# An LSTM stage of a graph network: the hidden state is computed on ACT, behind each tanh, in place of DVE

## The chip, the cores and the metric

One Trainium2 chip, one core. The metric is the device time of one execution in microseconds (us). Engines are named as the profile names them: PE is TensorE's matmuls, PEld its weight loads, DVE is VectorE, ACT is ScalarE, POOL is GpSimd, SP is SyncE.

## The reference, cut to what matters

The network has four levels, each a graph layer, a linear-attention layer and a feed-forward layer, on 625 nodes of 512 features. The feed-forward layer of the second level is an LSTM that runs over the 625 nodes as over time, with a batch of one:

```
def step(carry, x_t):
    h_prev, c_prev = carry
    combined = concatenate((x_t, h_prev))
    f_t = sigmoid(combined @ W_f + b_f)
    i_t = sigmoid(combined @ W_i + b_i)
    c_tilde = tanh(combined @ W_c + b_c)
    c_t = f_t * c_prev + i_t * c_tilde
    o_t = sigmoid(combined @ W_o + b_o)
    h_t = o_t * tanh(c_t)
    return (h_t, c_t), h_t
```

There are 625 such steps, and each needs the h of the one before. The part with x_t is computed for all nodes ahead of the loop; the part with h_prev is a product of one row of 512 by a 512 x 2048 matrix in each step.

## The kernel before, in words

Everything runs in one program, each engine with its own instruction stream, tied by semaphores. Of the four levels only the LSTM loop is touched. A sigmoid is computed as a tanh: with y = tanh(z/2), sigmoid(z) is (1 + y)/2, and the halves are folded into the weights. So the kernel's h is twice the reference's: h = (1 + y_o) * tanh(c).

The 512 hidden features lie as four columns (chunks) of 128 partitions in `ls_hid`. Two halves f = 0 and f = 1 of the features are treated one after the other, each with two chunks c = 0 and c = 1, so column 2f + c. Four semaphore events per step say that a column of h is new: `ls_h[0]` twice, `ls_h[1]` twice.

PE's step (L1153 to L1167): `seed(0)` and `seed(1)` put the x part of both halves into PSUM (L1143). Then come eight `add(f, c)` (L1149), each of which multiplies column c of h into the sums of half f, as 8 instructions. Their order is written out: (0,0), (1,0), (0,1), (0,2), (0,3), then (1,1), (1,2), (1,3). PE waits for column 0 before the first, for column 1 before (0,1), for column 2 (`ls_h[1]`) before (0,2) and for column 3 before (0,3). `add(0,3)` ends with `ls_full[0]`: half 0's sums are done. `add(1,3)` ends with `ls_full[1]`. `add(1,1)` ends with `ls_used`, column 1 having been read for the last time.

For each half DVE turns the sums from rows into columns: `turn` (L2225) for three of the gates and `turn_o` (L2230) for the output gate. ACT takes tanh of the three gates (L1607) and of the output gate (L1609, into `ls_gate[:, f, 8:10]`). DVE multiplies and adds: `product` (L2236), `cell` (L2241), `halve` (L2246). ACT takes the tanh of c, chunk by chunk, in two instructions with a per-partition bias (L1614, function `cell` on ACT). DVE then makes each column of h (L2255, function `hidden`). ACT's `keep` (L1619) copies the four columns to the output store, after both columns of half 1, and ACT's `pick_step` (L1624) prepares the seed's weights for the next step, at the start of a step.

Each engine handles its instructions in the order in which they are written. On DVE that order is `turn(0)`, `turn_o(0)`, `product(0)`, `cell(0)`, `hidden(0,0)`, `turn(1)`, `hidden(0,1)`, `turn_o(1)`, `halve(0)`, `product(1)`, `cell(1)`, `hidden(1,0)`, `hidden(1,1)`, `halve(1)`. On ACT it is pick, `gates(0)`, `cell(0)`, `gates(1)`, `cell(1)`, keep.

Beside the LSTM steps runs a sort of the 10,000 edges for the next level. In 320 of the 625 steps (two passes of 160) it puts eight small bf16 matmuls behind each step on PE (L1207), in every step one 625-element instruction on ACT behind `keep` (L1638 and L1643 in turn), and one large one on DVE in every second step (L2216). These are called rank steps here, and the other 305 plain steps. Between some of the plain steps stands a longer block of DVE work of the sort (L2339 to L2352 is one).

Of the kernel before, what the change touches and what calls it, by code (L numbers as in the profile page):

```python
# [26 lines left out]
ALU = mybir.AluOpType  # L27
ACT = mybir.ActivationFunctionType
# [176 lines left out]
def network(nc, io, last):  # L205
# [19 lines left out]
    with ExitStack() as ctx:  # L225
        def sb(name, shape, dt=F32):
            return ctx.enter_context(nc.sbuf_tensor(name, shape, dt))

        def sem(name):
            return ctx.enter_context(nc.semaphore(name))  # L230
# [32 lines left out]
        ls_hid = sb("ls_hid", [128, KC])  # L263
        ls_gate = sb("ls_gate", [128, 2, 10])
        ls_pr = sb("ls_pr", [128, 2, 4])
        ls_c = sb("ls_c", [128, 2, 2])
        ls_th = sb("ls_th", [128, 2, 2])
# [37 lines left out]
        ls_out_gate = [sem(f"ls_out_gate{f}") for f in range(2)]  # L305
        ls_prod = [sem(f"ls_prod{f}") for f in range(2)]
        ls_cell = [sem(f"ls_cell{f}") for f in range(2)]
        ls_tanh = [sem(f"ls_tanh{f}") for f in range(2)]
        wh_in = sem("wh_in")
        ls_h = [sem(f"ls_h{f}") for f in range(2)]  # L310
        ls_blank = sem("ls_blank")
        ls_used = sem("ls_used")
# [7 lines left out]
        ls_kept = sem("ls_kept")  # L320
# [89 lines left out]
        def weight(name):  # L410
            n = weight_at[name]
            _, k, w, _ = weights[n]
            return ring[:, n % RING, 0:k * w].rearrange("p (k w) -> p k w", k=k)
# [1069 lines left out]
        def _(act):  # L1483
# [70 lines left out]
            if last >= 3:  # L1554
# [5 lines left out]
                          bias=lambda c: cols[:, cb + c:cb + c + 1])  # L1560
# [18 lines left out]
            if last >= 4:  # L1579
# [8 lines left out]
                for i in range(4 * NT):  # L1588
                    t, j = i // 4, i % 4
# [21 lines left out]
                def cell(f, t):  # L1611
                    act.wait_ge(ls_prod[f], t + 1)
                    for c in range(2):
                        nc.scalar.activation(ls_th[:, f, c:c + 1], ls_pr[:, f, c:c + 1], ACT.Tanh, scale=0.5,  # L1614
                                             bias=ls_pr[:, f, 2 + c:3 + c]).then_inc(ls_tanh[f], 1)

                def keep(t):
                    act.wait_ge(ls_h[1], t * 2 + 4)
                    nc.scalar.activation(ls_out[:, :, bass.ds(t, 1)].rearrange("p c o -> p (c o)"), ls_hid[:, :],  # L1619
                                         ACT.Copy).then_inc(ls_kept, 1)  # L1620
# [5 lines left out]
                def step(t, last=False):  # L1626
                    if not last:
                        pick_step(t + 1)
                    gates(0, t)
                    cell(0, t)  # L1630
                    gates(1, t)
                    cell(1, t)
                    keep(t)
# [46 lines left out]
            if last >= 5:  # L1680
# [7 lines left out]
                          bias=lambda c: cols[:, bq + c:bq + c + 1])  # L1688
# [23 lines left out]
            def col(name, c):  # L1712
                return cols[:, COL_AT[name] + c:COL_AT[name] + c + 1]

            if last >= 6:
# [4 lines left out]
                for j in range(2):  # L1720
                    copy_cols(f"L2f.h{j}", lambda c: h1T[:, 4 * j + c, :], KC, ACT.Relu,
                              bias=lambda c: col("L2_ffn_b1", 4 * j + c))
            if last >= 7:
# [19 lines left out]
                for j in range(10):  # L1743
                    act.wait_ge(*made("L3.less", j // 5 + 1))
                    make(nc.scalar.activation(pT[j], sB[:, j // 5, :], ACT.Identity,
                                              bias=sdl[0:R, j // 5, j % 5:j % 5 + 1]), "L3.low")
# [38 lines left out]
        def _(dve):  # L1785
            st = Steps(dve, dve_step)
            V = nc.vector
# [347 lines left out]
            if last >= 4:  # L2135
# [49 lines left out]
                for i in range(4 * NT):  # L2185
                    t, j = i // 4, i % 4
# [36 lines left out]
                def turn(f, t, u):  # L2223
                    dve.wait_ge(ls_full[f], t + 1)
                    V.transpose(ls_turn[:, f, 2:8, :], ls_sum[u][f][:, 64:256].rearrange("p (g n) -> p g n", g=6)  # L2225
                                ).then_inc(ls_turned[f], 1)

                def turn_o(f, t, u):
                    dve.wait_ge(ls_full[f], t + 1)
                    V.transpose(ls_turn[:, f, 0:2, :], ls_sum[u][f][:, 0:64].rearrange("p (g n) -> p g n", g=2)  # L2230
                                ).then_inc(ls_turned_o[f], 1)

                def product(f, t):
                    dve.wait_ge(ls_sig[f], t + 1)
                    dve.wait_ge(ls_state[f], t + 1)
                    V.scalar_tensor_tensor(ls_pr[:, f, :], ls_gate[:, f, 0:4], 1.0, ls_gate[:, f, 4:8],  # L2236
                                           ALU.add, ALU.mult).then_inc(ls_prod[f], 1)

                def cell(f, t):
                    dve.wait_ge(ls_prod[f], t + 1)  # L2240
                    V.scalar_tensor_tensor(ls_c[:, f, :], ls_pr[:, f, 0:2], 0.5, ls_pr[:, f, 2:4],  # L2241
                                           ALU.mult, ALU.add).then_inc(ls_cell[f], 1)

                def halve(f, t):
                    dve.wait_ge(ls_cell[f], t + 1)
                    V.tensor_scalar(ls_gate[:, f, 6:8], ls_c[:, f, :], 0.5, None, ALU.mult).then_inc(ls_state[f], 1)  # L2246

                def hidden(f, c, t):
                    if c == 0:
                        dve.wait_ge(ls_out_gate[f], t + 1)  # L2250
                    if (f, c) == (0, 0):
                        dve.wait_ge(ls_kept, t + 1)
                        dve.wait_ge(ls_used, t + 1)
                    dve.wait_ge(ls_tanh[f], t * 2 + (c + 1))
                    V.scalar_tensor_tensor(ls_hid[:, 2 * f + c:2 * f + c + 1], ls_gate[:, f, 8 + c:9 + c], 1.0,  # L2255
                                           ls_th[:, f, c:c + 1], ALU.add, ALU.mult).then_inc(ls_h[f], 1)

                def step(t, u, between=None):
                    turn(0, t, u)
                    turn_o(0, t, u)  # L2260
                    product(0, t)
                    cell(0, t)
                    hidden(0, 0, t)
                    turn(1, t, u)
                    hidden(0, 1, t)
                    turn_o(1, t, u)
                    halve(0, t)
                    product(1, t)
                    cell(1, t)
                    if between:  # L2270
                        between()
                    hidden(1, 0, t)
                    hidden(1, 1, t)
                    halve(1, t)

                def rank_pass(k, t0):
                    with dve.Fori(0, ET // 2) as it:
                        for u in range(2):
                            step(it * 4 + (t0 + 2 * u), 0)
                            rank_place(it * 2 + (ET * k + u), u)  # L2280
                            step(it * 4 + (t0 + 2 * u + 1), 1, lambda: rank_put(it * 2 + (ET * k + u), u))

                def steps(a, b):
                    with dve.Fori(0, (b - a) // 2) as it:
                        for u in range(2):
                            step(it * 2 + (a + u), u)
                    if (b - a) % 2:
                        step(b - 1, 0)
# [483 lines left out]
```

## Time and profile before

| what | value |
|---|---|
| median of 3 runs | 4237.9 us (4237.68 to 4247.15) |
| profiled execution | 4236.93 us |
| its span (first to last instruction) | 4235.2 us |
| PE busy | 4087.3 us, 97% of the span |
| DVE busy | 2297.0 us, 54% |
| ACT busy | 1871.1 us, 44% |
| granted TensorE clock, mean | 0.976 |

The median is 1.0 us above the profiled execution, and that is 1.7 us above its span. A row of the page's list of costly groups reads: line, engine, operation, output<-inputs, shapes, count, then total busy time and mean ns of one, then the time for which the engine sat idle ahead of it, with what ended that. The share of PE is high partly because matmuls overlap and their ends are modelled: the start times of a step tell more.

### The profile page before, as it was taken

To read this page: it belongs to the slowest core of one execution; us is meant where nothing else is said; L and a number is where in the kernel's file an instruction comes from. 1 tells how busy PE (TensorE), PEld (TensorE's weight loads), DVE (VectorE), ACT (ScalarE), POOL (GpSimd) and SP (SyncE) were. 2 spreads that over 40 slices of the span, in tenths; PEclk is the share of its full clock that TensorE was granted. 3 is DMA by queue.
4 is the path that set the end of the run, shared out by engine and by line. 5 is a ranking of instruction groups with operands and counts; after the bars stand their busy time and mean duration, and the time that the engine had idled before them with its cause. 6 is when DMAs were issued, how large, how long until landed. Compare 5 with 4: busy or idle time off the path is not lost.

```text
span 4235.2 us, 138876 instructions
## 1 busy us (share of the span) xinstructions
PE 4087.3 (97%) x53914; PEld 2082.5 (49%) x53914; DVE 2297.0 (54%) x10694; ACT 1871.1 (44%) x7115; POOL 458.1 (11%) x452
## 2 busy tenths in 40 slices
PE   9999898999999999999999999999999999987999
PEld 7555454445555444445555444434444477456443
DVE  6444313666666666666666666666666145345212
ACT  0110111577777655577777655555555223030111
POOL 0000001000000123100000022200332100010321
PEclk9999899999999999999999999999999999998999
DMA  3010101630000000000000000000000141110974
GB/s 123 10 55 31 47 30 80 182 113 6 10 0 0 1 2 2 5 0 0 0 0 0 1 2 2 5 0 1 1 1 2 51 112 47 42 61 4 352 283 177
DMA packets 65113, 195.21 MB, mean 46 GB/s; under 512 B 29992, under 2 KB 37871, under 8 KB 49035
## 3 DMA queue, kind: packets, MB, share of 16 engines
q0 software_dynamic: 25824, 105.45, 7.8%
q1 hardware_dynamic: 39181, 88.23, 6.3%
q8 instruction: 78, 1.28, 0.1%
q14 instruction: 30, 0.25, 0.0%
HBM read 159.22 MB, written 34.15 MB: 46 GB/s over the span
## 4 chain that ended last, share of the span: by engine, by line
PE 94%; DVE 4%; ACT 1%; issue 1%; DMA 0%; POOL 0%; POOLq 0%; DVEq 0%; ACTq 0%
PE PS L1149 52%; PE PS L833 23%; PE PS L1432 4%; PE PS L1143 3%; PE PS L925 3%; PE PS L1207 2%; PE PS L1285 1%; PE PS L1333 1%; PE PS L1275 1%; PE PS L1265 1%; PE PS L864 1%; ACT BUF L1494 1%; PE PS L894 0%; DVE stats L1814 0%; PE PS L1428 0%
## 5 line engine op out<-in xcount | busy, mean ns | idle before, releaser
L1149 PE MATMUL PS<-BUF,ls_hid 128*1 128x256 f32 x40000 | 2309.0, 379 | 6.1 <-DVE ls_hid L2255 5.8
L1149 PEld LDWEIGHTS PS<-BUF,ls_hid 128*1 128x1 f32 x40000 | 955.2, 83 | 1155.5 <-DVE ls_hid L2255 299.1
L2225 DVE STREAM_TRANSPOSE ls_turn<-PS 128x192 f32<-128x192 f32 x1250 | 479.3, 383 | 466.5 <-PE PS L1149 466.2
L1614 ACT ACTIVATE ls_th<-ls_pr 128x1 f32<-128x1 f32 x2500 | 601.2, 287 | 102.1 <-DVE ls_pr L2236 0.2
L833 PE MATMUL PS<-ring,BUF 128*125 128x512 f32 (+1 forms) x1120 | 476.0, 583 | 13.0 <-ACT BUF L1494 5.7
L2255 DVE SCALAR_TENSOR_TENSOR ls_hid<-ls_gate,ls_th 128x1 f32<-128x1 f32 x2500 | 346.3, 150 | 229.9 <-ACT ls_th L1614 214.7
L1607 ACT ACTIVATE ls_gate<-ls_turn 128x6 f32<-128x6 f32 x1250 | 266.0, 213 | 318.7 <-DVE ls_turn L2225 238.9
L833 PEld LDWEIGHTS PS<-ring,BUF 128*125 128x125 f32 x1120 | 209.6, 190 | 265.5 <-issue 252.3
L1494 ACT ACTIVATE BUF<-PS 128x500 f32<-128x500 f32 (+1 forms) x100 | 50.6, 562 | 534.9 <-PE PS L864 438.0
L2230 DVE STREAM_TRANSPOSE ls_turn<-PS 128x64 f32<-128x64 f32 x1250 | 279.4, 224 | 0.0
L2236 DVE SCALAR_TENSOR_TENSOR ls_pr<-ls_gate 128x4 f32<-128x4 f32 x1250 | 215.2, 172 | 112.5 <-ACT ls_gate L1607 9.3
L1624 ACT ACTIVATE picked<-pick 128x1 bf16 x624 | 128.6, 206 | 298.0 <-PE PS L1149 276.6
L1143 PE MATMUL PS<-BUF,picked 126*1 126x256 bf16 (+1 forms) x5000 | 251.9, 272 | 8.7 <-ACT picked L1624 6.9
L1609 ACT ACTIVATE ls_gate<-ls_turn 128x2 f32<-128x2 f32 x1250 | 255.9, 205 | 0.0
L2241 DVE SCALAR_TENSOR_TENSOR ls_c<-ls_pr 128x2 f32<-128x2 f32 x1250 | 200.4, 160 | 42.7
L2246 DVE TENSOR_SCALAR ls_gate<-ls_c 128x2 f32<-128x2 f32 x1250 | 217.6, 174 | 0.2 <-issue 0.2
L1619 ACT ACTIVATE BUF<-ls_hid 128x4 f32 x625 | 130.9, 209 | 192.4 <-DVE ls_hid L2255 192.4
L738 POOL DMA_INDIRECT edges_by_cell<-duo x80 | 94.3, 1179 | 890.6 <-DVE ls_turn L2225 890.6
L833 PE MATMUL PS<-BUF,ring 128*128 128x113 f32 (+1 forms) x640 | 179.6, 442 | 3.0 <-ACT BUF L1494 2.1
L1143 PEld LDWEIGHTS PS<-BUF,picked 126*1 126x1 bf16 (+1 forms) x5000 | 112.6, 84 | 110.1 <-ACT picked L1624 7.9
L738 POOL DMA_INDIRECT edges_by_dst<-duo x80 | 94.5, 1181 | 527.5 <-issue 311.1
L1207 PE MATMUL PS<-AH,rows 125*32 125x512 bf16 (+3 forms) x2560 | 144.1, 297 | 0.0
(404 smaller groups left out, 3527.2 us busy)
## 6 DMA issues: line engine op xcount, KB each, us to landing
cell_bias<-BUF SPq DMA_DIRECT2D x5, 2441.4 KB
BUF<-cell_bias POOLq DMA_DIRECT2D x5, 2441.4 KB, 14.5
gate_inputs<-BUF SPq DMA_DIRECT2D x5, 1344.0 KB
rows_by_expert<-BUF POOLq DMA_DIRECT2D x1, 4352.0 KB, 29.3
BUF<-in_L_wh SPq DMA_DIRECT2D x4, 1024.0 KB, 12.9
ring<-in_L_w SPq DMA_DIRECT2D x4, 1024.0 KB, 4.8
expert_rows<-BUF SPq DMA_DIRECT2D x16, 256.0 KB, 2.3
BUF<-rows_by_expert SPq DMA_DIRECT2D x15, 256.0 KB, 7.4
```

What stands on the lines that cost most here:

```text
L833: ins = nc.tensor.matmul(out, a, b, start=(j == 0), stop=(j == len(terms) - 1))
L1143: nc.tensor.matmul(ls_sum[u][f][32 * q:32 * q + 1, :], picked[0:k, :], gx_tile[g][0:k, q, 2 * f:2 * f + 2, :, :].rearrange("p u j n -> p j ...
L1149: ins = nc.tensor.matmul(ls_sum[u][f][32 * q:32 * q + 1, :].rearrange("p (j n) -> p j n", j=4), ls_hid[:, c:c + 1], ls_half[:, q, c, :, f, :],
L1207: ins = nc.tensor.matmul(PS[p:e, 1, a:b], m[:, p:e], hot_rank[u][:, a:b], start=False, stop=False, skip_group_check=True)
L1607: nc.scalar.activation(ls_gate[:, f, 0:6], ls_turn[:, f, 2:8, 0], ACT.Tanh).then_inc(ls_sig[f], 1)
L1609: nc.scalar.activation(ls_gate[:, f, 8:10], ls_turn[:, f, 0:2, 0], ACT.Tanh).then_inc(ls_out_gate[f], 1)
L1614: nc.scalar.activation(ls_th[:, f, c:c + 1], ls_pr[:, f, c:c + 1], ACT.Tanh, scale=0.5, bias=ls_pr[:, f, 2 + c:3 + c]).then_inc(ls_tanh[f], 1)
L2225: V.transpose(ls_turn[:, f, 2:8, :], ls_sum[u][f][:, 64:256].rearrange("p (g n) -> p g n", g=6)).then_inc(ls_turned[f], 1)
L2230: V.transpose(ls_turn[:, f, 0:2, :], ls_sum[u][f][:, 0:64].rearrange("p (g n) -> p g n", g=2)).then_inc(ls_turned_o[f], 1)
L2236: V.scalar_tensor_tensor(ls_pr[:, f, :], ls_gate[:, f, 0:4], 1.0, ls_gate[:, f, 4:8], ALU.add, ALU.mult).then_inc(ls_prod[f], 1)
L2246: V.tensor_scalar(ls_gate[:, f, 6:8], ls_c[:, f, :], 0.5, None, ALU.mult).then_inc(ls_state[f], 1)
L2255: V.scalar_tensor_tensor(ls_hid[:, 2 * f + c:2 * f + c + 1], ls_gate[:, f, 8 + c:9 + c], 1.0, ls_th[:, f, c:c + 1], ALU.add, ALU.mult).the ...
```

## The change

The function `hidden` on DVE goes away. ACT's `cell` gets, behind each tanh, an ACTIVATE with the function Identity, whose scale is a column of per-partition values (the output gate's tanh) and whose bias is another (the tanh just made): y_o * tanh(c) + tanh(c), the same value as before. The waits that `hidden` had on DVE now stand on ACT, the one for the tanh included, which is now a wait of ACT for its own instruction.

```diff
                     for c in range(2):
                         nc.scalar.activation(ls_th[:, f, c:c + 1], ls_pr[:, f, c:c + 1], ACT.Tanh, scale=0.5,
                                              bias=ls_pr[:, f, 2 + c:3 + c]).then_inc(ls_tanh[f], 1)
+                        if c == 0:
+                            act.wait_ge(ls_out_gate[f], t + 1)
+                        if (f, c) == (0, 0):
+                            act.wait_ge(ls_kept, t + 1)
+                            act.wait_ge(ls_used, t + 1)
+                        act.wait_ge(ls_tanh[f], t * 2 + (c + 1))
+                        nc.scalar.activation(ls_hid[:, 2 * f + c:2 * f + c + 1], ls_th[:, f, c:c + 1], ACT.Identity,
+                                             scale=ls_gate[:, f, 8 + c:9 + c], bias=ls_th[:, f, c:c + 1]).then_inc(ls_h[f], 1)
...
-                def hidden(f, c, t):
-                    if c == 0:
-                        dve.wait_ge(ls_out_gate[f], t + 1)
-                    if (f, c) == (0, 0):
-                        dve.wait_ge(ls_kept, t + 1)
-                        dve.wait_ge(ls_used, t + 1)
-                    dve.wait_ge(ls_tanh[f], t * 2 + (c + 1))
-                    V.scalar_tensor_tensor(ls_hid[:, 2 * f + c:2 * f + c + 1], ls_gate[:, f, 8 + c:9 + c], 1.0,
-                                           ls_th[:, f, c:c + 1], ALU.add, ALU.mult).then_inc(ls_h[f], 1)
-
                 def step(t, u, between=None):
                     turn(0, t, u)
                     turn_o(0, t, u)
                     product(0, t)
                     cell(0, t)
-                    hidden(0, 0, t)
                     turn(1, t, u)
-                    hidden(0, 1, t)
                     turn_o(1, t, u)
                     halve(0, t)
                     product(1, t)
                     cell(1, t)
                     if between:
                         between()
-                    hidden(1, 0, t)
-                    hidden(1, 1, t)
                     halve(1, t)
```

## Rows read from the trace of the kernel before

**Rows 1.** The page's head: span, and busy time by engine

```profile
span 4235.2 us, 138876 instructions
PE 4087.3 (97%) x53914; PEld 2082.5 (49%) x53914; DVE 2297.0 (54%) x10694; ACT 1871.1 (44%) x7115; POOL 458.1 (11%) x452
```

**Rows 2.** The chain that ended last: shares by engine and by line

```profile
PE 94%; DVE 4%; ACT 1%; issue 1%; DMA 0%; POOL 0%; POOLq 0%; DVEq 0%; ACTq 0%
PE PS L1149 52%; PE PS L833 23%; PE PS L1432 4%; PE PS L1143 3%; PE PS L925 3%; PE PS L1207 2%; PE PS L1285 1%; PE PS L1333 1%; PE PS L1275 1%; PE PS L1265 1%; PE PS L864 1%; ACT BUF L1494 1%; PE PS L894 0%; DVE stats L1814 0%; PE PS L1428 0%
```

**Rows 3.** The page's costliest groups (columns as described above)

```profile
L1149 PE MATMUL PS<-BUF,ls_hid 128*1 128x256 f32 x40000 | 2309.0, 379 | 6.1 <-DVE ls_hid L2255 5.8
...
L1614 ACT ACTIVATE ls_th<-ls_pr 128x1 f32<-128x1 f32 x2500 | 601.2, 287 | 102.1 <-DVE ls_pr L2236 0.2
...
L2255 DVE SCALAR_TENSOR_TENSOR ls_hid<-ls_gate,ls_th 128x1 f32<-128x1 f32 x2500 | 346.3, 150 | 229.9 <-ACT ls_th L1614 214.7
```

**Rows 4.** Line L1619 (keep): count, ns min/median/max, first and last start

```profile
L1619 ACT ACTIVATE BUF<-ls_hid x625: 208/209/213, 811.4 to 3281.7; 128x4 f32 x154, 128x4 f32<-128x4 f32 x3
```

**Rows 5.** Timeline, ACT, a plain step: start, us, instruction, [idle before <-releaser]

```profile
2601.78 0.21 ACT L1607 ACTIVATE ls_gate<-ls_turn 128x6 f32<-128x6 f32 x1
...
2602.22 0.48 ACT L1614 ACTIVATE ls_th<-ls_pr 128x1 f32<-128x1 f32 x2
2603.08 0.21 ACT L1607 ACTIVATE ls_gate<-ls_turn 128x6 f32<-128x6 f32 x1 [0.37 <-DVE ls_turn L2225]
...
2603.57 0.48 ACT L1614 ACTIVATE ls_th<-ls_pr 128x1 f32<-128x1 f32 x2
2604.36 0.21 ACT L1619 ACTIVATE BUF<-ls_hid 128x4 f32 x1 [0.31 <-DVE ls_hid L2255]
```

**Rows 6.** Timeline, DVE, the same plain step

```profile
2601.36 0.38 DVE L2225 STREAM_TRANSPOSE ls_turn<-PS 128x192 f32<-128x192 f32 x1 [0.80 <-PE PS L1149]
...
2602.55 0.16 DVE L2255 SCALAR_TENSOR_TENSOR ls_hid<-ls_gate,ls_th 128x1 f32<-128x1 f32 x1 [0.17 <-ACT ls_th L1614]
2602.66 0.38 DVE L2225 STREAM_TRANSPOSE ls_turn<-PS 128x192 f32<-128x192 f32 x1
...
2603.32 0.21 DVE L2236 SCALAR_TENSOR_TENSOR ls_pr<-ls_gate 128x4 f32<-128x4 f32 x1
2603.57 0.16 DVE L2241 SCALAR_TENSOR_TENSOR ls_c<-ls_pr 128x2 f32<-128x2 f32 x1
2603.97 0.28 DVE L2255 SCALAR_TENSOR_TENSOR ls_hid<-ls_gate,ls_th 128x1 f32<-128x1 f32 x2 [0.24 <-ACT ls_th L1614]
...
2605.29 0.38 DVE L2225 STREAM_TRANSPOSE ls_turn<-PS 128x192 f32<-128x192 f32 x1 [0.81 <-PE PS L1149]
```

**Rows 7.** Timeline, weight loads of PE, the same plain step

```profile
2602.76 0.97 PEld L1149 LDWEIGHTS PS<-BUF,ls_hid 128*1 128x1 f32 x24 [0.25 <-DVE ls_hid L2255]
2604.18 0.10 PEld L1149 LDWEIGHTS PS<-BUF,ls_hid 128*1 128x1 f32 x8 [0.45 <-DVE ls_hid L2255]
```

**Rows 8.** Timeline, PE, a rank step

```profile
2204.71 0.45 PE L1207 MATMUL PS<-AH,rows 125*32 125x512 bf16 x8
2204.98 0.40 PE L1143 MATMUL PS<-BUF,picked 120*1 120x256 bf16 x8
2205.20 3.63 PE L1149 MATMUL PS<-BUF,ls_hid 128*1 128x256 f32 x64
2208.66 0.45 PE L1207 MATMUL PS<-AH,rows 125*32 125x512 bf16 x8
```

**Rows 9.** ACT's groups by shape: the rank instruction, and a table load

```profile
L1638 ACT ACTIVATE AH<-iota,AH 125x625 f32<-125x625 f32 x160 | 130.9, 818 | 0.8 <-DVE AH L2297 0.8
...
L1494 ACT ACT_TABLE_LOAD x1 | 1.3, 1283 | 0.8 <-PEq L2762 0.8
```

**Rows 10.** Windows around a DVE block: us, busy by engine, PEclk, DMA, GB/s

```profile
2848.00:2855.00 7.00, 4.00 (x76) 1.50 (x68) 6.48 (x20) 1.33 (x7) 0.00 (x0) 1.00 0.00 0
2855.00:2862.00 7.00, 4.78 (x48) 1.52 (x52) 2.14 (x15) 3.67 (x11) 0.00 (x0) 0.53 0.00 0
```

## The prediction, made before the changed kernel was built or run

> **What bounds the kernel now.** I read the page's head first: PE is busy for 97% of the span, DVE for 54%, ACT for 44% [rows 1]. The chain of waits agrees: 94% of it is PE, and the matmuls with h (L1149) are 52% of the span alone [rows 2]. That alone would say that ACT and DVE have room and that moving small work between them is free. The start times say something else, so the timeline of single steps is the view that decides.
>
> `keep` runs once a step, first at 811.4 us and last at 3281.7 us [rows 4]: 624 periods in 2470.3 us, 3.96 us each, blocks between steps included. In a rank step PE is full: 8 adds take 2208.66 - 2205.20 = 3.46 us (0.43 each), the rank matmuls 0.27 and the seeds 0.22, together 3.95 us, which is the whole distance between two starts of L1207 [rows 8]. In a plain step PE would need 3.46 + 0.22 = 3.68 us, but two starts of `turn(0)` lie 3.93 us apart [rows 6]. The rest is waiting for h: the weight loads stood 0.25 us before column 0 and 0.45 us before column 2, released by DVE's L2255 both times [rows 7] (part of that is covered by matmuls still running). So the plain steps are bound by a ring of latencies through PE, DVE and ACT, and the rank steps by PE with that ring close behind. A delay of one column of h by more than some 0.1 us goes into every step.
>
> **The ring before, in a plain step**, counted from the start of `turn(0)` (2601.36) [rows 5, 6]: tanh of the gates at 0.42, first tanh of c at 0.86, h column 0 begun at 1.19 on DVE; `turn(1)` at 1.30, tanh of half 1's gates at 1.72, tanh of its c at 2.21, column 2 begun at 2.61 and column 3 done at 2.89. PE starts on column 2 at 2.82 [rows 7], which is 0.05 after that column is done (2603.97 + 0.16 = 2604.13). `add(0,3)` comes one add later, at 3.25, and the next `turn(0)` at 3.93, so 0.68 after the start of `add(0,3)`. What matters: ACT is idle from the end of half 0's two tanh (1.34) until half 1's gates (0.37 us idle) [rows 5], and DVE makes h there.
>
> **What is removed.** 2500 DVE instructions of 0.15 us [rows 3] leave DVE. Worth nothing by itself: DVE waits 0.80 us for PE before each `turn(0)`, and `turn(1)` begins at 2602.66, beside and not behind h (it is PE's event that releases it). The handoff from ACT to DVE is also gone, and this is where a gain would have to come from. DVE's L2255 started 0.33 us after its tanh of 0.29 [rows 3, 5, 6], so the handoff is 0.04 us. But the new instruction still waits for the tanh's semaphore on its own engine. The rows show one such wait on DVE: `product` starts at 2603.32 and takes 0.21, and both DVE's own `cell` and ACT's tanh start at 2603.57 [rows 5, 6], 0.04 behind its end. Own engine and other engine cost the same. So I take no gain: the new ACTIVATE starts 0.33 us behind the first tanh of a pair, 0.32 behind the second (which is 0.28 long), and 0.40 behind half 1's first one, where two waits have to be passed (2603.57 to 2603.97) [rows 6].
>
> **What the new instruction costs.** No row shows an ACTIVATE with both scale and bias from memory. Without such an operand a tiny one takes 0.209 us [rows 4], and the tanh with a bias of that kind 0.287 [rows 3]: one operand costs 0.08. If the second costs as much, the new one takes 0.37. Bounds: 0.21 if neither costs anything, 0.29 if the second is free; upward 0.48, the time of the whole pair of tanh [rows 5]. I take 0.37, which is also the middle, since the kind of operand and not the function explains the difference between the rows. The Trainium skill (page "ScalarE: Activation LUTs", section "What ACT_TABLE_LOAD costs") says that an ACTIVATE with immediates takes 186 ns, and that each [128,1] pointer operand adds about 93 ns. By it the instruction would take 372 ns, and the sum would be about 5 us larger.
>
> What follows an ACTIVATE starts before its end: the pair of tanh lasts 0.48 for two of 0.29 [rows 3, 5], so 0.09 are overlapped. The new one holds ACT for 0.28.
>
> **The ring after.** ACT's order is now tanh, h, tanh, h, with waits in between that nothing can pass. Half 0: tanh at 0.86, h column 0 at 1.19 (done 1.56, before 1.35), tanh at 1.47, column 1 at 1.79 (done 2.16), ACT free for the next at 2.07. Queued behind it are half 1's gates. They were ready at 1.72, so they start 0.35 late, and with them everything of half 1. From the gates' tanh to the tanh of c took 0.44 (0.42 to 0.86), so the latter is at 2.51. Column 2 begins at 2.91, done 3.28; tanh at 3.19; column 3 at 3.51, done 3.88. PE's `add(0,3)` needs column 3: 3.93. Before, column 3 was hidden behind the add of column 2; now it comes 0.60 after column 2 and the add covers only 0.43, so it is column 3 that decides. Next `turn(0)` 0.68 later: 4.61 us.
>
> PE in a rank step: `turn(0)` starts 0.68 after `add(0,3)` starts, so that add and the three behind it end at 1.04, rank matmuls and seeds at 1.53; column 0 is usable at 1.61, columns 0 and 1 feed three adds until 2.90, then PE waits until 3.33 for column 2 and until 3.93 for column 3. It would be the same 4.61, and the PE bound of 3.95 plays no part any more. ACT in a rank step: `keep` starts 0.11 behind column 3 (2604.25 to 2604.36) at 3.99, the 0.82 instruction at about 4.13, and ends at 4.95, that is 0.34 into the next period. `pick` overlaps its end by 0.09 and takes 0.21 less 0.08, so the gates' tanh could start at 0.38; they are due at 0.42. It just fits, with 0.04 to spare; if not, the rank steps pay the difference. POOL's scatters wait for a turn each and only get more time.
>
> **The sum.** Plain steps 305 x (4.61 - 3.93) = 207 us; rank steps 320 x (4.61 - 3.95) = 211 us. The few blocks of DVE work between steps begin earlier in the longer step (DVE has its last column work behind `cell(1)`, no longer behind column 3), which gives back under 1 us each: -3. Profiled execution 4236.9 + 415 = 4652; the median was 1.0 above. Forecast: 4653 us.
>
> **Rivals.**
> *A, the second operand is free.* The new instruction takes 0.29. All four lie in the ring, so 0.32 less: 4.29, and 305 x 0.36 + 320 x 0.34 = 219, less 3: 4453. For it: nothing but that no row has both. Against: the first one costs 0.08.
> *B, each wait costs more on ACT.* Before `keep` ACT starts 0.11 and not 0.04 after what it waits for [rows 5, 6]. If the same holds for three of the four new instructions (the fourth has 0.11 in it already), it is 0.21 x 625 = 131 more: 4784. Against: `keep` writes to an address that moves with the step, the new one doesn't.
> *C, faster.* ACT does not really wait for its own tanh: h starts 0.20 behind it, as the second tanh does, and takes 0.29. Then half 0 holds ACT until 0.86 + 4 x 0.20 = 1.66, before 1.72; half 1's tanh of c is at 2.16, column 2 done at 2.65, PE starts at 2.70 instead of 2.82, column 3 is done at 3.05 and hidden again. Plain steps 3.81, rank steps stay at PE's 3.95: 305 x -0.12 = -37, 4201 us. It decides where the new instruction starts under 0.20 behind the tanh; the wait for `ls_tanh` in the code and DVE's own 0.04 speak against it.
> *D, no change.* It takes 0.21, as if neither operand cost anything: 0.64 off the ring, 3.97, bounded by PE: at most 305 x 0.04 + 320 x 0.02 = 19, about 4250. The tanh's 0.287 speaks against it.
> *E, something coarser.* PE idles 0.7 to 0.9 us per step, and the granted clock might fall: at 1.2 GHz a plain step needs 7.4 us and the whole some 6550. In the 7 us around a block of DVE work PE was busy for 4.00 us; the clock was 1.00 in them and 0.53 in the next 7 [rows 10]; the new pauses are all under 0.5 us. A table load of 1.28 us [rows 9] between Tanh and Identity would be of the same order. There are four in the whole trace, and none between the Identity of the level above, L1559, and the loop's first tanh. The Trainium skill (the same page, section "Table sets: the hidden batching unit") says that cheap functions, identity among them, are in every set; the trace agrees so far.
>
> **How the numbers follow.** Forecast with its own range of 4590 to 4710: 0.66. A 0.13, B and a longer instruction 0.13, C 0.02, D 0.03, E 0.03. The range from 4440 to 4800 takes in A and most of B. A measurement can tell 0.3% (13 us) here. Faster 0.02 (C), within 0.3% 0.02 (most of D), slower 0.96.
>
> **What would show it.** L2255 is gone from DVE; a new group of 2500 on ACT at about 370 ns; ACT's idle before L1607 of half 1 gone, and that tanh starting some 0.77 behind `turn(1)`'s start instead of 0.42; two starts of `turn(0)` 4.6 apart in plain and rank steps alike; weight loads of L1149 waiting for ACT; clock 1.00 in the loop. I would be wrong if the new group is far from 370 ns, if it starts less than 0.3 behind its tanh, or if the periods of plain and rank steps still differ.

## The result, and the profile after

| | before | changed |
|---|---|---|
| median | 4241.9 us (4 runs, 4237.68 to 4247.15) | 4669.5 us (4 runs, 4665.28 to 4670.52) |
| ratio | | 1.1002, 95% interval 1.0989 to 1.1015 |
| span of the profiled execution | 4235.2 us | 4667.6 us |
| forecast | | 4653 us (4440 to 4800) |

10% slower, as forecast, 16 us above the forecast. The page's head after the change answers to [rows 1]:

```profile
span 4667.6 us, 138868 instructions
PE 4321.7 (93%) x53914; PEld 1974.7 (42%) x53914; DVE 2064.6 (44%) x8194; ACT 2668.7 (57%) x9615; POOL 457.8 (10%) x452
```

ACT is busy for 798 us more, DVE for 232 us less, and the span is 432 us longer. No engine but PE comes near its limit by this view, and PE's share fell. The chain of waits (shares by engine, then by line) says what took over:

```profile
PE 49%; ACT 29%; DVE 11%; issue 9%; POOL 1%; DMA 0%; ACTq 0%; POOLq 0%; DVEq 0%
PE PS L833 21%; PE PS L1149 17%; ACT ls_th L1614 12%; ACT ls_hid L1622 11%; DVE ls_pr L2244 5%; ACT ls_gate L1607 4%; PE PS L1432 4%; DVE ls_turn L2233 3%; PE PS L925 2%; PE PS L1285 1%; ACT picked L1632 1%; PE PS L1333 1%; PE PS L1275 1%; PE PS L1265 1%; PE PS L864 1%
```

Before, PE made up 94% of it and the matmuls with h 52% [rows 2]; now L1149 is 17%, and the two kinds of ACT instructions behind `product` are 23%. That is the picture of a ring in which PE waits. From the page's costliest groups (columns as in [rows 3]):

```profile
L1149 PEld LDWEIGHTS PS<-BUF,ls_hid 128*1 128x1 f32 x40000 | 846.7, 83 | 1696.1 <-ACT ls_hid L1622 987.8
L1622 ACT ACTIVATE ls_hid<-ls_th,ls_gate 128x1 f32<-128x1 f32 x2500 | 967.9, 387 | 121.7
```

The new instruction takes 387 ns (0.37 us was forecast), and it is what the weight loads wait for in more than half of their idle time (987.8 of 1696.1 us). Line L1627 is `keep`, once a step; its row answers to [rows 4]:

```profile
L1627 ACT ACTIVATE BUF<-ls_hid x625: 208/211/213, 811.7 to 3713.6; 128x4 f32 x154, 128x4 f32<-128x4 f32 x3
```

The loop, from the first to the last of them, takes 2901.9 us and before 2470.3: 431.6 of the 432.4 us by which the span grew. Practically all of it is in the loop. One plain step on ACT (timeline: start, us, instruction), answering to [rows 5]:

```profile
2831.49 0.21 ACT L1607 ACTIVATE ls_gate<-ls_turn 128x6 f32<-128x6 f32 x1
...
2831.93 0.29 ACT L1614 ACTIVATE ls_th<-ls_pr 128x1 f32<-128x1 f32 x1
2832.26 0.39 ACT L1622 ACTIVATE ls_hid<-ls_th,ls_gate 128x1 f32<-128x1 f32 x1
2832.55 0.28 ACT L1614 ACTIVATE ls_th<-ls_pr 128x1 f32<-128x1 f32 x1
2832.86 0.39 ACT L1622 ACTIVATE ls_hid<-ls_th,ls_gate 128x1 f32<-128x1 f32 x1
2833.15 0.20 ACT L1607 ACTIVATE ls_gate<-ls_turn 128x6 f32<-128x6 f32 x1
...
2833.58 0.29 ACT L1614 ACTIVATE ls_th<-ls_pr 128x1 f32<-128x1 f32 x1
2833.97 0.39 ACT L1622 ACTIVATE ls_hid<-ls_th,ls_gate 128x1 f32<-128x1 f32 x1
2834.26 0.28 ACT L1614 ACTIVATE ls_th<-ls_pr 128x1 f32<-128x1 f32 x1
2834.57 0.39 ACT L1622 ACTIVATE ls_hid<-ls_th,ls_gate 128x1 f32<-128x1 f32 x1
2835.07 0.21 ACT L1627 ACTIVATE BUF<-ls_hid 128x4 f32 x1
```

And DVE's turns and PE's weight loads of the same step, answering to [rows 6] and [rows 7]:

```profile
2831.07 0.38 DVE L2233 STREAM_TRANSPOSE ls_turn<-PS 128x192 f32<-128x192 f32 x1 [1.51 <-PE PS L1149]
...
2832.36 0.38 DVE L2233 STREAM_TRANSPOSE ls_turn<-PS 128x192 f32<-128x192 f32 x1 [0.28 <-PE PS L1149]
...
2835.69 0.38 DVE L2233 STREAM_TRANSPOSE ls_turn<-PS 128x192 f32<-128x192 f32 x1 [1.51 <-PE PS L1149]
```

```profile
2832.69 0.97 PEld L1149 LDWEIGHTS PS<-BUF,ls_hid 128*1 128x1 f32 x24 [0.47 <-ACT ls_hid L1622]
2834.41 0.10 PEld L1149 LDWEIGHTS PS<-BUF,ls_hid 128*1 128x1 f32 x8 [0.74 <-ACT ls_hid L1622]
2835.01 1.40 PEld L1149 LDWEIGHTS PS<-BUF,ls_hid 128*1 128x1 f32 x32 [0.50 <-ACT ls_hid L1622]
```

Read them from the first turn, 2831.07, as zero. Half 1's turn comes at 1.29 (before: 1.30), and its gates' tanh, which was at 1.72, comes at 2.08: it stands in ACT's queue behind tanh, h, tanh, h of half 0, which run from 0.86 to 2.18 without a gap that anything could use. PE, which before did five adds in one go from column 2 on (40 weight loads from 2604.18, of which [rows 7] shows the first 8), now stops once more, for column 3 (2835.01, 0.60 behind column 2). The next turn is at 4.62, where it was at 3.93. The granted clock was 1.00 in both of two long stretches of the loop (windows; the fourth field from the right is PEclk):

```profile
1600.00:1950.00 350.00, 318.30 (x5448) 117.92 (x5440) 158.34 (x757) 261.89 (x1060) 81.36 (x69) 1.00 0.05 2
2000.00:2350.00 350.00, 332.08 (x6052) 131.46 (x6048) 175.06 (x869) 306.42 (x1136) 0.00 (x0) 1.00 0.00 0
```

The first stretch is of plain and the second of rank steps. ACT is busy for 0.88 of the rank stretch and still does not bind it: two rank steps' `keep` are 4.62 apart, too (2404.48 and 2409.10):

```profile
2404.48 0.21 ACT L1627 ACTIVATE BUF<-ls_hid 128x4 f32 x1
2404.60 0.82 ACT L1646 ACTIVATE AH<-iota,AH 125x625 f32<-125x625 f32 x1
2405.32 0.19 ACT L1632 ACTIVATE picked<-pick 128x1 bf16 x1
2405.51 0.21 ACT L1607 ACTIVATE ls_gate<-ls_turn 128x6 f32<-128x6 f32 x1
...
2409.10 0.21 ACT L1627 ACTIVATE BUF<-ls_hid 128x4 f32 x1
```

### The profile page after: what moved, and what is told of

The parts are those of the page before. It is cut to its first block, busy times and chain, and to the rows that moved or that the text cites. A ratio compares the mean times of both kernels' runs of the same rounds, so it can differ in the third digit from the quotient of the medians.

```text
span 4667.6 us, 138868 instructions
## 1 busy us (share of the span) xinstructions
PE 4321.7 (93%) x53914; PEld 1974.7 (42%) x53914; DVE 2064.6 (44%) x8194; ACT 2668.7 (57%) x9615; POOL 457.8 (10%) x452
## 4 chain that ended last, share of the span: by engine, by line
PE 49%; ACT 29%; DVE 11%; issue 9%; POOL 1%; DMA 0%; ACTq 0%; POOLq 0%; DVEq 0%
PE PS L833 21%; PE PS L1149 17%; ACT ls_th L1614 12%; ACT ls_hid L1622 11%; DVE ls_pr L2244 5%; ACT ls_gate L1607 4%; PE PS L1432 4%; DVE ls_turn L2233 3%; PE PS L925 2%; PE PS L1285 1%; ACT picked L1632 1%; PE PS L1333 1%; PE PS L1275 1%; PE PS L1265 1%; PE PS L864 1%
## 5 line engine op out<-in xcount | busy, mean ns | idle before, releaser
L1149 PE MATMUL PS<-BUF,ls_hid 128*1 128x256 f32 x40000 | 2497.9, 379 | 204.9 <-ACT ls_hid L1622 204.8
L1149 PEld LDWEIGHTS PS<-BUF,ls_hid 128*1 128x1 f32 x40000 | 846.7, 83 | 1696.1 <-ACT ls_hid L1622 987.8
L1622 ACT ACTIVATE ls_hid<-ls_th,ls_gate 128x1 f32<-128x1 f32 x2500 | 967.9, 387 | 121.7
L1614 ACT ACTIVATE ls_th<-ls_pr 128x1 f32<-128x1 f32 x2500 | 718.1, 287 | 152.4 <-DVE ls_pr L2244 0.2
L2244 DVE SCALAR_TENSOR_TENSOR ls_pr<-ls_gate 128x4 f32<-128x4 f32 x1250 | 203.7, 163 | 383.3 <-ACT ls_gate L1607 293.1
L1607 ACT ACTIVATE ls_gate<-ls_turn 128x6 f32<-128x6 f32 x1250 | 255.1, 204 | 46.5 <-DVE ls_turn L2233 3.9
L2238 DVE STREAM_TRANSPOSE ls_turn<-PS 128x64 f32<-128x64 f32 x1250 | 258.2, 207 | 0.0
L2254 DVE TENSOR_SCALAR ls_gate<-ls_c 128x2 f32<-128x2 f32 x1250 | 239.0, 191 | 16.2
L1609 ACT ACTIVATE ls_gate<-ls_turn 128x2 f32<-128x2 f32 x1250 | 245.3, 196 | 0.0
L1627 ACT ACTIVATE BUF<-ls_hid 128x4 f32 x625 | 131.7, 211 | 73.2 <-ACT ls_hid L1622 7.7
L1766 ACT ACTIVATE AC<-PS 128x512 f32<-128x512 f32 x51 | 30.5, 597 | 227.1 <-PE PS L1432 227.1
```

Source lines behind the costliest of these rows:

```text
L1149: ins = nc.tensor.matmul(ls_sum[u][f][32 * q:32 * q + 1, :].rearrange("p (j n) -> p j n", j=4), ls_hid[:, c:c + 1], ls_half[:, q, c, :, f, :],
L1607: nc.scalar.activation(ls_gate[:, f, 0:6], ls_turn[:, f, 2:8, 0], ACT.Tanh).then_inc(ls_sig[f], 1)
L1609: nc.scalar.activation(ls_gate[:, f, 8:10], ls_turn[:, f, 0:2, 0], ACT.Tanh).then_inc(ls_out_gate[f], 1)
L1622: nc.scalar.activation(ls_hid[:, 2 * f + c:2 * f + c + 1], ls_th[:, f, c:c + 1], ACT.Identity, scale=ls_gate[:, f, 8 + c:9 + c], bias=ls_t ...
```

## The experiments

The theory, called ring: the time is a ring of latencies through PE, DVE and ACT, and h on ACT costs what it adds to that ring, by its length, by its wait and by what stands behind it. The main rival, called work: each h made on ACT costs the same, wherever it stands, since ACT has more to do. "Loop" below is the time from the first to the last `keep` of the profiled execution: 2470.3 us before, 2901.9 changed. It leaves out what happens outside the loop. The median of the kernel before was 4245 to 4250 us in these comparisons, and the run with the best loop, taken twice (before_gate_wait_early and gate_wait_early), had loops of 2450.5 and 2450.4 us.

| run | median, us | ratio to before (95% interval) | loop, us | loop against before |
|---|---|---|---|---|
| pairs_first | 4384.2 | 1.0326 (1.0308 to 1.0345) | 2620.5 | +150.2 |
| half0_on_act | 4385.2 | 1.0333 (1.0314 to 1.0352) | 2617.3 | +147.0 |
| half1_on_act | 4415.5 | 1.0402 (1.0382 to 1.0421) | 2651.1 | +180.8 |
| column3_on_act | 4242.1 | 0.9990 (0.9980 to 1.0000) | 2473.4 | +3.1 |
| no_operands | 4247.3 | 1.0003 (0.9992 to 1.0013) | 2479.5 | +9.2 |
| one_operand | 4438.4 | 1.0452 (1.0434 to 1.0470) | 2671.6 | +201.3 |
| no_wait_for_tanh | 4279.4 | 1.0083 (1.0066 to 1.0100) | 2510.9 | +40.6 |
| gate_wait_early_on_act | 4625.3 | 1.0892 (1.0876 to 1.0909) | 2863.2 | +392.9 |
| before_gate_wait_early | 4213.3 | 0.9925 (0.9911 to 0.9939) | 2450.5 | -19.8 |
| gate_wait_early | 4214.7 | 0.9922 (0.9909 to 0.9935) | 2450.4 | -19.9 |
| gate_wait_early_halve_late | 4214.7 | 0.9920 (0.9907 to 0.9933) | 2450.5 | -19.8 |

**Where h stands on ACT.**

```diff
+                    for c in range(2):            # a second loop: both h behind both tanh
                         if c == 0:
                             act.wait_ge(ls_out_gate[f], t + 1)
...
```

> Same instructions as the changed kernel, but on ACT both tanh of a half stand ahead of both h. Theory ring (the time is the ring of latencies through PE, DVE and ACT; what counts is how long ACT is held before half 1's gates, and when column 3 is ready): the first h starts 0.39 behind the first tanh (0.20 for the second tanh, 0.19 until ACT takes the next), the second 0.29 later and is done at 1.07; ACT is free 0.97 behind the first tanh instead of 1.22. Half 1's tanh of c comes 0.25 earlier, column 3 is done 1.08 behind it instead of 1.38. Column 3 is hidden behind the add of column 2 again: period 4.22 us, about 4412 us in all. Rival work (each h on ACT costs the same 0.17 us wherever it stands, as ACT has more to do): as the changed kernel, 4669 us.

The same instructions in another order give back 281 of the 431.6 us in the loop. Work said none; ring said 4412 us, 28 more than measured. One step on ACT:

```profile
3353.38 0.22 ACT L1607 ACTIVATE ls_gate<-ls_turn 128x6 f32<-128x6 f32 x1
...
3353.83 0.48 ACT L1614 ACTIVATE ls_th<-ls_pr 128x1 f32<-128x1 f32 x2
3354.22 0.65 ACT L1623 ACTIVATE ls_hid<-ls_th,ls_gate 128x1 f32<-128x1 f32 x2
3354.77 0.20 ACT L1607 ACTIVATE ls_gate<-ls_turn 128x6 f32<-128x6 f32 x1
```

From half 0's to half 1's gates it is 1.39 us instead of 1.66. The wait for the first tanh is filled by the second one. ACT was held for 0.94 (3353.83 to 3354.77) where 0.97 was expected, and column 3 was done 1.06 instead of 1.08 behind half 1's first tanh (3355.20, and 3355.59 + 0.67). That is 0.05 a step, and accounts for the 28.

**Which half.** Only one half's h on ACT, the other's on DVE as before.

```diff
+                        if (f, c) in ((0, 0), (0, 1)):     # half1_on_act: ((1, 0), (1, 1))
+                            ...                            # the waits and the ACTIVATE of the change
...
-                    hidden(0, 0, t)                    # half1_on_act: hidden(1, 0, t) and hidden(1, 1, t)
-                    hidden(0, 1, t)
```

> Only half 0's two columns of h are made on ACT; half 1's stay on DVE. Theory ring: ACT is held 1.22 behind half 0's first tanh, half 1's gates start at 2.08 in the step instead of 1.72, their tanh of c at 2.52, column 2 (DVE) done at 3.08, column 3 hidden: period 4.24, about 4420 us (+183). Rival work: half of the changed kernel's loss, 4454 us (+216). If the two parts only add up, this and the run with half 1 on ACT make +432 together; the ring gives less, 408, because column 3 is hidden in this one.

> Only half 1's two columns of h are made on ACT; half 0's stay on DVE. Theory ring: half 1's gates start in time (1.72), its tanh of c at 2.17, column 2 begins at 2.58, the next tanh at 2.87, column 3 at 3.18 and is done at 3.57; PE's add of it starts at 3.62 instead of 3.25: period 4.30, about 4462 us (+225), larger than for half 0. Rival work: +216, 4454 us. What tells them apart is the timeline: with the ring, PE waits before column 3 and not before column 2 by more than 0.3 us.

They are 35 and 47 us under what the ring gave, the order between them is right, and work's 4454 us is out by 69 and 39. PE's weight loads tell the two apart, first with half 0, then with half 1 on ACT:

```profile
3351.04 0.97 PEld L1149 LDWEIGHTS PS<-BUF,ls_hid 128*1 128x1 f32 x24 [0.47 <-ACT ls_hid L1623]
3352.47 1.83 PEld L1149 LDWEIGHTS PS<-BUF,ls_hid 128*1 128x1 f32 x40 [0.46 <-DVE ls_hid L2264]
```

```profile
3353.58 0.97 PEld L1149 LDWEIGHTS PS<-BUF,ls_hid 128*1 128x1 f32 x24 [0.25 <-DVE ls_hid L2264]
3355.15 0.11 PEld L1149 LDWEIGHTS PS<-BUF,ls_hid 128*1 128x1 f32 x8 [0.60 <-ACT ls_hid L1623]
3355.75 1.40 PEld L1149 LDWEIGHTS PS<-BUF,ls_hid 128*1 128x1 f32 x32 [0.50 <-ACT ls_hid L1623]
```

With half 0 on ACT, columns 2 and 3 go through in one piece (x40), late as a whole. With half 1 on ACT, column 3 is waited for on its own. What the sum had too large in both is the 0.40 that I put between half 1's tanh and its h: here it was 0.33 (in half1_on_act, tanh at 3354.38 and h at 3354.71; in half0_on_act, 3351.92 and 3352.25). That is 0.07 x 625 = 44 us. The two together make 328 us, the change 432: not additive, and by 104 us instead of the 24 expected. Most of the gap is this same wait: it is 0.40 in the kernel before and 0.39 in the changed one, so each of the two runs gains 0.07 on it and the changed kernel 0.01, which makes 0.13 x 625 = 81 us. No run isolates the rest, some 20 us. An estimate: rank steps were held by PE and not by the ring, so that each run alone may use up once what the ring had to spare there.

**Only column 3.** A semaphore of its own (ls_h3) keeps its event apart from column 2's, which DVE gives.

```diff
+                        if (f, c) == (1, 1):
+                            act.wait_ge(ls_out_gate[f], t + 1)
+                            act.wait_ge(ls_tanh[f], t * 2 + (c + 1))
+                            nc.scalar.activation(ls_hid[:, 3:4], ls_th[:, f, c:c + 1], ACT.Identity,
+                                                 scale=ls_gate[:, f, 9:10], bias=ls_th[:, f, c:c + 1]).then_inc(ls_h3, 1)
...
-                    hidden(1, 1, t)
```

> Only column 3, the last of the step, is made on ACT, behind both tanh of half 1, with a semaphore of its own; columns 0, 1 and 2 stay on DVE. ACT's h costs the same 0.39 us here, but nothing waits behind it on ACT, and it is done 0.98 behind half 1's first tanh (0.20 for the second tanh, 0.39 until its end and the wait, 0.39), at 3.19, while PE is ready for it at 3.25. Theory ring: no change, 4238 us, within 5. Rival work: a quarter of the loss, +108, 4346 us.

No change: loop +3.1 us, where work said +108. The instruction is as long as in the changed kernel:

```profile
L1620 ACT ACTIVATE ls_hid<-ls_th,ls_gate 128x1 f32<-128x1 f32 x625 | 241.6, 387 | 21.7 <-ACT ls_th L1615 0.4
```

So 387 ns on ACT cost nothing where only `keep` stands behind them and PE is not yet ready for the column. Work is refuted.

**What makes the instruction long, and what its length costs.**

```diff
-                                             scale=ls_gate[:, f, 8 + c:9 + c], bias=ls_th[:, f, c:c + 1]).then_inc(ls_h[f], 1)
+                                             scale=1.5).then_inc(ls_h[f], 1)       # one_operand: scale=1.5, bias=ls_th[...]
```

> The changed kernel, with the constant 1.5 as the scale of the new ACTIVATE and no bias: h = 1.5 tanh(c), so the output gate is left out. All waits stay. It measures the two operands that come from memory. Theory ring: the instruction takes 0.21 instead of 0.39; four of them are in the ring, so the period falls by 0.71 from 4.63 to 3.92 and is then held by PE, 3.95 in rank steps: 4237 to 4250 us, no change from the kernel before. Rival (the waits for its own tanh and ACT's order cost the time, the length of the instruction does not matter): still above 4500 us.

> The changed kernel, with the constant 1.5 as the scale and the tanh as bias from memory: h = 2.5 tanh(c), the output gate is left out. Theory ring: the instruction takes 0.30, the period is 4.63 - 4 x 0.09 = 4.28, about 4449 us. If the first operand costs nothing and the second all, it is 4237 to 4250 us; if the first costs all, 4669 us.

Both kernels leave out the output gate. First without, then with one operand from memory:

```profile
L1622 ACT ACTIVATE ls_hid<-ls_th 128x1 f32<-128x1 f32 x2500 | 507.4, 203 | 117.7
```

```profile
L1622 ACT ACTIVATE ls_hid<-ls_th 128x1 f32<-128x1 f32 x2500 | 737.8, 295 | 119.8
```

203, 295, 387 ns for none, one, two: 92 each, and the two cost the same. The loops are 2479.5, 2671.6 and 2901.9. From one to two operands the loop grows by 230.3 us; 4 x 0.092 x 625 = 230: all four instructions of a step stand in the ring, and their length alone accounts for the difference. From none to one it is only 192. Without operands the rank steps end at PE's own time (3.94 us between two starts of `turn(0)`, the median of 320), and in the plain ones (3.96) column 3 follows column 2 by 0.42 and is hidden behind its add again. And without the operands the whole change costs 9 us in the loop, with every wait and ACT's order as they are. So there is no loss without the two operands, and it is the order that puts all four instructions in the ring.

The Trainium skill (page "ScalarE: Activation LUTs", section "What ACT_TABLE_LOAD costs") puts a [128,1] pointer operand at about 93 ns. The trace agrees, with 92 for each of two; the whole instruction took 387, where an estimate from the page's terms gives 372.

**The wait for its own tanh.** The h reads the tanh's inputs.

```diff
-                        act.wait_ge(ls_tanh[f], t * 2 + (c + 1))
-                        nc.scalar.activation(ls_hid[:, 2 * f + c:2 * f + c + 1], ls_th[:, f, c:c + 1], ACT.Identity,
-                                             scale=ls_gate[:, f, 8 + c:9 + c], bias=ls_th[:, f, c:c + 1]).then_inc(ls_h[f], 1)
+                        nc.scalar.activation(ls_hid[:, 2 * f + c:2 * f + c + 1], ls_pr[:, f, c:c + 1], ACT.Identity,
+                                             scale=ls_gate[:, f, 8 + c:9 + c], bias=ls_pr[:, f, 2 + c:3 + c]).then_inc(ls_h[f], 1)
```

> The changed kernel, where the new ACTIVATE reads the tanh's inputs (ls_pr, both as input and as bias) instead of the tanh, so that it has nothing to wait for; the tanh is still computed and not used, so h is wrong on that point: h = y_o * a + b in place of (1 + y_o) * tanh. Order and operands as in the changed kernel. It measures the wait for an instruction of its own engine. Theory ring: each h starts 0.20 behind its tanh instead of 0.33, ACT is held 0.98 instead of 1.22, column 3 done 1.1 behind half 1's first tanh instead of 1.38: period 4.09, about 4331 us. Theory that only the longer instruction costs: near 4669 us.

```profile
3101.56 0.29 ACT L1614 ACTIVATE ls_th<-ls_pr 128x1 f32<-128x1 f32 x1
3101.76 0.37 ACT L1621 ACTIVATE ls_hid<-ls_pr,ls_gate 128x1 f32<-128x1 f32 x1
3102.04 0.28 ACT L1614 ACTIVATE ls_th<-ls_pr 128x1 f32<-128x1 f32 x1
3102.23 0.38 ACT L1621 ACTIVATE ls_hid<-ls_pr,ls_gate 128x1 f32<-128x1 f32 x1
3102.51 0.20 ACT L1607 ACTIVATE ls_gate<-ls_turn 128x6 f32<-128x6 f32 x1
```

h starts 0.20 and 0.19 behind its tanh, not 0.33 and 0.31, and is 372 ns long. The loop is +40.6 us instead of +431.6. Forecast was +94, a period of 4.09 us, and it was 4.00: ACT is held 0.95 and not 0.98, the tanh of c follows the gates in 0.42 instead of 0.44, and column 3 is done 1.04 and not 1.1 behind half 1's first tanh (3102.93, and 3103.60 + 0.37). Column 3 still decides, though only just: PE's weight loads of it start 0.46 behind those of column 2 (3103.56 and 3104.02), and one add covers 0.43. So the length and the wait are not two shares of one sum: either of them away gives back most of it, 422 and 391 us. The kernel before had this wait as well, as DVE's for ACT's tanh, so this run takes away more than the change put in. Had ACT not waited, the change would still not have been faster.

**A wait that costs more than others.** The changed kernel, then the kernel before, with the wait for half 1's output gate taken where the engine is idle:

```diff
+                    if f == 1:                                    # on ACT: ahead of half 1's first tanh
+                        act.wait_ge(ls_out_gate[f], t + 1)
...
+                    if f == 1:                                    # on DVE: ahead of cell(1)
+                        dve.wait_ge(ls_out_gate[f], t + 1)
                     dve.wait_ge(ls_prod[f], t + 1)
...
-                    if c == 0:
+                    if (f, c) == (0, 0):
                         dve.wait_ge(ls_out_gate[f], t + 1)
```

> The changed kernel, where ACT's wait for half 1's output gate stands ahead of half 1's first tanh instead of behind it. In the changed kernel's trace the h of column 0 starts 0.33 behind its tanh and that of column 2 0.39; in the run with only half 1 on ACT it was 0.33. Theory: the 0.06 is the sequencer passing the tanh's semaphore in an instruction of its own, which comes when two waits stand in that order; with one left it is 0.33. The ring gives 0.06 less in all 625 steps, plain and rank alike: about 4630 us (-39). Rival: the wait ahead of the tanh delays the tanh by as much: 4669 us.

> The kernel before, where DVE's wait for half 1's output gate stands ahead of cell(1) instead of hidden(1,0); nothing else differs. In the kernel before, the h of column 2 starts 0.40 behind its tanh and that of column 0 only 0.33: two waits have to be passed. With one of them taken earlier, where DVE is idle anyway, column 2 should be ready 0.07 earlier. Theory ring: a plain step falls from 3.93 to 3.86 and rank steps stay at PE's 3.95: -21 us, about 4217. Rival (half 0's column 0 binds the plain steps as well, or the wait costs as much ahead of cell): no change, 4238 us.

On ACT the loop falls by 38.7 us against the changed kernel, 0.062 a step, as forecast; h now starts 0.33 behind half 1's first tanh (3353.17 and 3353.50):

```profile
3353.17 0.29 ACT L1616 ACTIVATE ls_th<-ls_pr 128x1 f32<-128x1 f32 x1
3353.50 0.39 ACT L1624 ACTIVATE ls_hid<-ls_th,ls_gate 128x1 f32<-128x1 f32 x1
```

On DVE, in the kernel before, the plain step falls from 3.93 to 3.85 us (two starts of `turn(0)`), and h starts 0.58 behind `product(1)` instead of 0.65 [rows 6]:

```profile
3100.25 0.38 DVE L2225 STREAM_TRANSPOSE ls_turn<-PS 128x192 f32<-128x192 f32 x1 [0.73 <-PE PS L1149]
...
3102.20 0.21 DVE L2236 SCALAR_TENSOR_TENSOR ls_pr<-ls_gate 128x4 f32<-128x4 f32 x1
3102.52 0.16 DVE L2243 SCALAR_TENSOR_TENSOR ls_c<-ls_pr 128x2 f32<-128x2 f32 x1
3102.78 0.34 DVE L2257 SCALAR_TENSOR_TENSOR ls_hid<-ls_gate,ls_th 128x1 f32<-128x1 f32 x2
...
3104.10 0.38 DVE L2225 STREAM_TRANSPOSE ls_turn<-PS 128x192 f32<-128x192 f32 x1 [0.74 <-PE PS L1149]
```

`cell(1)` starts later for it, which nobody waits for. The loop gains 19.8 us, as forecast. This is the fastest kernel of the study, 0.75% under the one before. By the medians it is 35 us, but by the profiled executions 20.7 (spans of 4235.2 and 4214.5), nearly all of it in the loop. The other 15 go with the clock granted to the kernel before: the executions with a mean of 0.972 or 0.973 took 4249 to 4254 us, the one with 0.978 took 4233, and this kernel took 4210 to 4211 with 0.978.

> The same kernel as before_gate_wait_early once more, beside the next one on the same chip: 20 to 35 us under the kernel before.

It came out the same, 0.9922.

```diff
                     turn_o(1, t, u)
-                    halve(0, t)
...
                     hidden(1, 1, t)
+                    halve(0, t)
                     halve(1, t)
```

> before_gate_wait_early, with DVE's halve(0) moved from ahead of product(1) to the end of the step. In plain steps product(1) takes 0.21 us and in rank steps 0.16. If it is halve(0) right ahead of it that lengthens it, a plain step falls from 3.85 to 3.81 us, where PE's wait for column 0 sets the end: about 12 us less than before_gate_wait_early. Rival: the 0.21 has another cause (the runs without operands show it too, with halve(0) further ahead): no change against before_gate_wait_early.

The first reading was wrong and the rival right: no change, and `product(1)` still takes 0.21 in plain steps, with `halve(0)` gone from ahead of it:

```profile
3101.43 0.21 DVE L2236 SCALAR_TENSOR_TENSOR ls_pr<-ls_gate 128x4 f32<-128x4 f32 x1
3101.44 1.17 POOL L738 DMA_INDIRECT cell_bias<-AH  x1 [2.67 <-DVE ls_turn L2225]
```

The second row shows what it goes with. In 222 of the 305 plain steps POOL begins a scatter 12 to 29 ns behind the start of `product(1)`, here and in the kernel before. In these `product(1)` takes 206 to 223 ns; the other 1028 `product` take 161 to 166, but for one of 270 in the kernel before. In the changed kernel the scatters of 222 steps begin 0.3 us ahead of `product(1)`, and it takes 161 to 165 ns there. No run takes the scatter away, so that it is the cause is likely and not shown.

## Why the prediction was right

The time, the sign and the mechanism were as predicted; the forecast of the loop's growth was 415 us and it was 431.6. Step by step:

- *No gain from the removed handoff.* Right. Behind a tanh of 0.29, h starts at 0.33 on ACT as it did on DVE. The wait of ACT for itself cost as much here as that of DVE for ACT (medians of 0.328 and 0.327 from the first tanh to its h), and no_wait_for_tanh shows what it is worth when it is really gone.
- *Length 0.37.* It was 0.387, the term of the sum that was furthest off: four in the ring make 0.07 a step, 43 us too little in the sum. The rule from the two rows of before (0.209 without, 0.287 with one operand, so 0.08 each) was right in kind, but took the difference between two different instructions; with the same instruction it is 0.092. The two operands being equally dear, which rival A denied, is shown by one_operand.
- *ACT held until 2.07, half 1's gates 0.35 late.* 2.08 and 0.36. The gates' tanh to the tanh of c took 0.43 (2833.15 to 2833.58) and not 0.44, and half 1's h came 0.39 and not 0.40 behind it; such hundredths gave back most of the longer instruction, so that the period came to 4.63 (the median of plain and of rank steps alike) against 4.61. Two of these terms were luck. The 0.44 was half 0's; half 1's own was 0.49 [rows 5], and it fell to 0.43 because `product(1)` no longer took 0.21, for which the prediction gave no reason. And the 0.40 was carried over from DVE to ACT, while the same lines took 0.33 in half1_on_act. The first was worth 0.05 in 222 steps, 11 us, the second 0.07 in all of them, some 40.
- *Column 3 decides instead of column 2.* Right: PE's weight loads wait 0.50 us for it on their own, which they did not before.
- *Rank steps end at the same period as plain ones, and ACT's 0.82 instruction just fits.* Right; two `keep` of rank steps are 4.62 apart with the 0.82 instruction between them, and plain steps 4.62, too. The gates' tanh still starts 0.42 behind `turn(0)` in 318 of the 320 rank steps.
- *The blocks.* Plain steps with a longer block exceed the others by 16 us in all before and by 13 changed (counted where the excess is over 0.3 us): 3 given back, as forecast.
- *Clock and table loads.* 1.00 in both stretches of the loop, and no tables between Tanh and Identity.
- Rival A would have been right with one operand (4438 measured, 4453 in its sum) and rival D with none (4247, about 4250 in its sum). Rival C was not run as a whole (no wait and a short instruction together); without the wait alone the change is still slower. Rival B (each wait dearer on ACT) holds for one of the four, where it had been counted.

## What to carry to other kernels

In a loop that carries a dependency, read the start times of one period before the busy shares: a half-idle engine can still be full at the moment that counts. Moving a small operation to the engine that made its input saves no handoff as long as it has to wait for that input, and what is queued behind it waits, too. An ACTIVATE of one element per partition cost almost double with a scale and a bias from memory (387 ns for 203); and where an instruction waits for two events, try to take the earlier one where the engine is idle, which was worth 0.06 to 0.07 us a step in both kernels.

## What the runs showed of the hardware that was not expected

- An ACTIVATE of one element: 203 ns without, 295 with one, 387 with two operands from memory. In the run without the wait it was 372 with two.
- Two waits ahead of one instruction cost 0.06 us more or nothing, with the same code for one column: 0.39 between half 1's tanh and its h in the changed kernel, 0.33 where only half 1 was on ACT. The Trainium skill (page "Perfetto Trace Analysis", section "Identifying Dependency Chains") says that an instruction that waits on several engines may have EventSemaphore instructions put ahead of it. The traces agree: where it took 0.39, the tanh's semaphore was waited for in such an instruction, 60 to 64 ns ahead of the ACTIVATE, in all 625 steps of the changed kernel; where it took 0.33, the ACTIVATE carried it itself, in all but 9 steps of half1_on_act. DVE's 0.40 in the kernel before has such an instruction as well, 66 ns ahead. The rows of ACT's sequencer for the line of that wait, in the changed kernel and then in half1_on_act (the changed kernel's 634 have 9 of half 0):

```profile
L1621 ACTq EVENT_SEMAPHORE  x634: 17/17/38, 810.5 to 3712.5; - x159
```

```profile
L1622 ACTq EVENT_SEMAPHORE  x9: 17/17/17, 1465.8 to 3460.8; - x9
```

- `product` took 0.21 us instead of 0.16 in those 222 steps in which a scatter of POOL began 12 to 29 ns behind its start, and 0.16 where the scatter began 0.3 us ahead of it.
